# Graph layer on one Trainium2 core: first relu in halves, rank base ahead of the transposes, counts from a column of ones, means on ScalarE in the last phase, last store cut

## The chip, the cores and the metric

One Trainium2 chip, one core of it. The metric is the device time of the whole kernel in microseconds (us).

## The reference

A layer of a graph network on 3,125 nodes of 64 features with 53,125 edges (sorted by destination), float32:

```python
h = relu(layernorm(x))
msg = concatenate([h[dst], edge_attr], axis=1)      # per edge
m = relu(msg @ W1a.T + b1a) @ W1b.T + b1b           # hidden 128
agg = segment_sum(m, src) / maximum(counts(src), 1) # mean per node
z = relu(concatenate([h, agg]) @ W2a.T + b2a) @ W2b.T + b2b
out = x + concatenate([z, h]) @ Wr.T + br
```

## The kernel before

The second matmul of an edge is linear, so the kernel averages the relu'd hidden rows per source node and applies the combined weights `wc` to the mean.

**Edges.** They come in 52 groups of 1,024 (8 tiles of 128), and two groups are a pair. For a pair PE projects windows of `h` (L861), ScalarE copies them into `pw` (L758), DVE makes a one-hot of the destination within a window (`onehot`, L512), and `hidden(g)` (L912) multiplies edges and one-hot with `pw` in 8 calls (16 matmul instructions) into two PSUM banks. `relu(g)` (L766) writes the result into a payload buffer `pay`, one of `PB` = 4.

**Ranks.** The hidden rows must be brought together by source node. Nodes lie in 25 buckets of 125. PE counts for every edge how many edges of its bucket came before it: `ranks_from` (L873) sets the PSUM bank `RANK` to the base of each bucket's region, `ranks_before` and `ranks_on` (both through `count_on`, L876) add counts. DVE's `ranks_b` makes slot numbers of it (L492 to L504, the last being `pos_i`), and writes the node's place in its bucket, 1 to 125, as `MARK` behind the 128 hidden values. POOL then writes each tile with one indirect DMA, a scatter, into `slots_dram` (L411): 8 per group, 416 in all, after `pos` and `rl` of the group. A row there has 144 floats. Regions are cleared beforehand by SP's DMAs (L296), since padding rows must have mark 0. Reuse of a payload buffer waits for its scatters (L500 on DVE, L765 on ScalarE).

**Phases.** The pairs are cut into phases of 8, 8, 6, 3 and 1. When a phase's scatters have landed, its regions are read back bucket by bucket in rounds: SP loads rows (L331, four buffers in turn), DVE compares marks with 1 to 125 (`hots`, L523), PE multiplies (L928, `sum_round`), DVE adds to `sums` (L538). A planner at the top of the function spreads rounds over the group loop by counts of matmuls. What is left comes after the loop (`left_over`).

**The last phase** is nine tails, eight of 3 buckets and one of 1. Each engine writes its order out by hand, in software pipeline. For iteration q, PE does `sum_round(q)`, `transposes(q-1)` (L983), `z1(q-2)` (L993), `outs(q-3)` (L1001). DVE does `hots(q+1)`, `take_tail(q)` (L643 total, L648 to L650 count and reciprocal, L651 mean), `add_z(q-2)` (L660), `add_out(q-3)` (L665). ScalarE copies the transposed mean (L808, for q) and does the relu of z (L814, for q-2). Before, the sum of the column `MARK` is the place times the count, so the count is found with `rec_mark` (reciprocals of 1 to 125) and rounding by `MAGIC`.

**The head.** PE's order is: `transpose_h(0)` (L846), `project_windows(0)` (L861), `ranks_from(0)`, `ranks_before(0)`, `hidden(0)`. SP issues loads and clears in one written order; its load of `dst` for group 3 stands behind many of them.

**Stores.** SP stores the output after tails 3, 6 and 9, each as two DMAs (`HALVES`: partitions 0 to 111 and 112 to 124), L353. A fallback for unusual inputs follows a flag and isn't entered here.

Of the kernel before, what the change touches and what calls it, by code (L numbers as in the profile page):

```python
# [7 lines left out]
def gnn_layer(nc, x_chunks, x, src_cols, dst, dst_blocks, dst_cols, edges_T, w_early, w_late, out):  # L8
# [4 lines left out]
    HID = 128  # L13
# [39 lines left out]
    RW, SW = HID + 16, HID + 1  # L53
    MARK = HID
# [12 lines left out]
    for ph in range(NPH):  # L67
        m = min(3, TPR // C[ph])
        for b0 in range(0, NB, m):
            sum_rounds.append(("sum", ph, b0, min(m, NB - b0)))  # L70
# [37 lines left out]
    with ExitStack() as ctx:  # L108
# [3 lines left out]
        def sem(name):  # L112
# [7 lines left out]
        rec_mark = sb("rec_mark", [128, 1])  # L120
# [88 lines left out]
            oh="onehot_made", H="hidden_made", rl="hidden_relu", pos="slots_ready",  # L209
# [4 lines left out]
            sb="mean_made", sT="mean_transposed", sTe="mean_T_evacuated", z="z_made", za="z_added", zr="z_relu",  # L214
# [48 lines left out]
        OUT_AT = [3, 6, NJ]  # L263
# [4 lines left out]
        def _(sp):  # L268
# [80 lines left out]
            for upto in OUT_AT:  # L349
                hi = tails[upto - 1][1] + tails[upto - 1][2]  # L350
                sp.wait_ge(S["oe"], upto)
                for p0, p1 in HALVES:
                    sp.dma_start(o_v[p0:p1, lo:hi, :], ot[p0:p1, lo:hi, :]).then_inc(S["out"], 16)  # L353
                lo = hi
            sp.wait_ge(S["out"], 16 * len(OUT_AT) * len(HALVES))
# [12 lines left out]
        def _(pool):  # L368
# [29 lines left out]
            count(rec_mark[:], [[0, 1]], 1, 1)  # L398
# [3 lines left out]
            for g in range(NG):  # L402
# [6 lines left out]
                pool.wait_ge(S["rl"], g + 1)  # L409
                for k in range(K):  # L410
                    pool.indirect_dma_start(out=slots_dram[:, :], out_offset=bass.IndirectOffsetOnAxis(ap=pos_i[:, u, k:k + 1], axis=0),  # L411
# [16 lines left out]
        def _(dve):  # L428
# [33 lines left out]
            V.memset(pay[:].rearrange("p u k w -> p (u k) w")[:, :, SW:RW], 0.0).then_inc(S["pad"], 1)  # L462
# [52 lines left out]
            def hots(r):  # L515
# [6 lines left out]
                for t in range(m * C[ph]):  # L522
                    last = V.tensor_scalar(oh2[:, r % 2, t, :], marks[:], rows[:, sum_no[r] % RR, t, MARK:SW], None, ALU.is_equal)  # L523
# [67 lines left out]
            for i in range(NP):  # L591
# [8 lines left out]
                if i == 0:  # L600
# [5 lines left out]
                    dve.wait_ge(S["const"], 4)  # L606
                    link(V.reciprocal(rec_mark[:], rec_mark[:]))
# [32 lines left out]
            def take_tail(q):  # L640
                r, b0, m = tails[q]
                dve.wait_ge(S["ag"], r + 1)
                V.tensor_tensor(tot[:, q % 2, 0:m, :], sums[:, b0:b0 + m, :], summed(r), ALU.add).then_inc(S["tk"], 1)  # L643
                dve.wait_ge(S["tk"], r + 1)
                if q >= 2:
                    dve.wait_ge(S["sT"], q - 1)
                c = cnt[:, q % 2]
                link(V.tensor_scalar(c[:, 0:m, 0], tot[:, q % 2, 0:m, MARK], rec_mark[0:BN, :], MAGIC, ALU.mult, ALU.add))  # L648
                link(V.tensor_scalar(c[:, 0:m, 1], c[:, 0:m, 0], -MAGIC, 1.0, ALU.add, ALU.max))
                link(V.reciprocal(c[:, 0:m, 2], c[:, 0:m, 1]))  # L650
# [447 lines left out]
```

## Time and profile before

| | us |
|---|---|
| median of 3 runs | 594.39 (594.15 to 594.48) |
| profiled execution, its own time | 594.85 |
| span of the profiled execution | 593.1 |
| POOL busy, 442 instructions | 408.2 (69%) |
| PE matmul busy | 383.1 (65%) |
| PE weight load busy | 344.5 (58%) |
| DVE busy | 318.1 (54%) |
| ACT busy | 100.2 (17%) |
| mean granted clock of TensorE | 0.805 |

PE is TensorE (PEld its weight loads, which overlap), DVE is VectorE, ACT ScalarE, POOL GpSimd, SP the engine that issues most DMAs (SPq its queue). The 1.7 us between span and time lie around the span. Shares are of the whole span; what one stage is worth must be read in that stage.

### The profile page before, as it was taken

The page shows a single profiled execution, that of the slowest core. Times are in us where ns is not written, and L with a number is a line of the kernel's source. Part 1 is how long each engine was busy: PE and PEld are TensorE (multiplying, and loading weights), DVE is VectorE, ACT ScalarE, POOL GpSimd, SP SyncE. Part 2 cuts the span into 40 slices and gives each one's busy share as a digit, 9 for nine tenths or more (in the row PEclk, how much of TensorE's full clock was granted, in tenths as well). Part 3 has the DMA queues.
Part 4 walks back from the last instruction along what each step waited for, and adds up shares of the span by engine and source line. Part 5 has one row for each costly group of instructions (what it writes and reads, how often), then busy time and mean ns, then how long its engine had stood idle before and what let it go on. Part 6 is the DMA issues. An engine that isn't in the chain of part 4 may idle for free.

```text
span 593.1 us, 7898 instructions
## 1 busy us (share of the span) xinstructions
PE 383.1 (65%) x2608; PEld 344.5 (58%) x2608; DVE 318.1 (54%) x1237; ACT 100.2 (17%) x145; POOL 408.2 (69%) x442
## 2 busy tenths in 40 slices
PE   5546947976255267378468551763985928897875
PEld 3445847745145267378457551663875928797754
DVE  6658422334233346357446432562765818888895
ACT  2241511112122021022112220211221211100022
POOL 2677777777777777777777777777777777777000
PEclk9775957678676596788789765968896978999999
DMA  8982845363443695677675647858697594969511
GB/s 195 362 233 88 243 136 170 92 187 101 124 132 125 186 290 182 215 242 228 221 230 161 180 137 234 247 184 255 200 305 235 165 309 126 323 216 315 177 38 57
DMA packets 54637, 116.35 MB, mean 196 GB/s; under 512 B 9869, under 2 KB 30949, under 8 KB 54593
## 3 DMA queue, kind: packets, MB, share of 16 engines
q1 hardware_dynamic: 41281, 85.11, 47.8%
q0 software_dynamic: 13312, 30.70, 16.2%
q8 instruction: 22, 0.36, 0.3%
q14 instruction: 22, 0.18, 0.1%
HBM read 68.62 MB, written 47.14 MB: 195 GB/s over the span
## 4 chain that ended last, share of the span: by engine, by line
POOL 42%; issue 18%; PE 15%; DMA 11%; DVE 7%; SPq 3%; ACT 2%; POOLq 0%; DVEq 0%; ACTq 0%
POOL slots_dram L411 42%; DMA slots_dram<-pay,pos_i 7%; PE bank L912 6%; PE bank L928 5%; DVE oh L523 3%; DMA dstb<-in_dst 2%; DMA rows<-slots_dram 2%; ACT pay L766 1%; PE bank L1001 1%; DVE eo L512 1%; PE bank L876 1%; PE bank L861 1%; SPq L272 1%; PE bank L932 1%; ACT z1T L814 1%
## 5 line engine op out<-in xcount | busy, mean ns | idle before, releaser
L411 POOL DMA_INDIRECT slots_dram<-pay,pos_i x416 | 404.2, 972 | 139.5 <-issue 123.5
L912 PE MATMUL bank<-pw,eo 128*128 128x128 f32 x832 | 142.7, 343 | 166.9 <-DVE eo L512 166.1
L912 PEld LDWEIGHTS bank<-pw,eo 128*128 128x128 f32 x832 | 134.4, 253 | 176.5 <-issue 176.1
L928 PE MATMUL bank<-rows,oh 128*125 128x129 f32 x1050 | 126.0, 275 | 9.8 <-DVE oh L523 9.6
L928 PEld LDWEIGHTS bank<-rows,oh 128*125 128x125 f32 x1050 | 119.7, 188 | 13.7 <-issue 12.9
L766 ACT ACTIVATE pay<-bank 128x1024 f32<-128x1024 f32 x52 | 53.3, 1024 | 409.1 <-PE bank L912 407.9
L523 DVE TENSOR_SCALAR oh<-marks,rows 128x125 f32<-128x125 f32 x525 | 108.1, 293 | 3.1 <-DMA rows<-slots_dram 2.5
L501 DVE COPY pay<-mark 128x8 f32<-128x8 f32 x52 | 10.6, 214 | 142.8 <-DMA slots_dram<-pay,pos_i 142.1
L512 DVE TENSOR_SCALAR eo<-dstb,lane 64x256 f32<-64x256 int32 x208 | 64.0, 367 | 6.0 <-DMA dstb<-in_dst 5.2
L492 DVE TENSOR_TENSOR slot_t<-bank,eq 128x416 f32<-128x416 f32 x26 | 15.3, 590 | 48.7 <-PE bank L876 47.4
L861 PE MATMUL bank<-we_in,hT 65*128 65x128 f32 x208 | 38.5, 347 | 0.7 <-ACT hT L751 0.7
L861 PEld LDWEIGHTS bank<-we_in,hT 65*128 65x128 f32 x208 | 36.8, 265 | 1.6 <-issue 1.1
L758 ACT COPY pw<-bank 64x512 f32<-64x512 f32 x52 | 30.0, 578 | 11.2 <-PE bank L861 10.4
L538 DVE TENSOR_TENSOR sums<-sums,bank 125x258 f32<-125x258 f32 (+2 forms) x48 | 20.5, 428 | 13.3 <-PE bank L928 13.3
L876 PE MATMUL bank<-fours,all_rows 128*128 128x312 bf16 (+1 forms) x156 | 24.1, 265 | 0.0
L876 PE MATMUL bank<-eq,below 128*128 128x416 bf16 x26 | 9.6, 371 | 16.2 <-DVE fours L488 16.2
L876 PEld LDWEIGHTS bank<-fours,all_rows 128*128 128x128 bf16 x156 | 14.8, 104 | 1.7
L494 DVE TENSOR_REDUCE pos<-slot_t 128x16 f32<-128x416 f32 x26 | 15.2, 586 | 0.9
L484 DVE TENSOR_TENSOR eq<-srcq,bucket_row 128x416 bf16<-128x416 f32 x26 | 15.2, 586 | 0.4
L876 PE MATMUL bank<-eq,all_rows 128*128 128x208 bf16 x52 | 14.6, 280 | 0.0
L876 PEld LDWEIGHTS bank<-eq,below 128*128 128x128 bf16 x26 | 2.6, 102 | 20.1 <-DVE fours L488 17.1
L876 PE MATMUL bank<-twos,all_rows 128*128 128x208 bf16 x52 | 14.3, 274 | 0.0
(138 smaller groups left out, 225.4 us busy)
## 6 DMA issues: line engine op xcount, KB each, us to landing
rows<-slots_dram SPq DMA_DIRECT2D x24, 864.0 KB, 7.5
dstb<-in_dst SPq DMA_DIRECT2D x52, 256.0 KB, 8.5
eo<-in_edges_T SPq DMA_DIRECT2D x52, 256.0 KB, 3.8
rows<-slots_dram SPq DMA_DIRECT2D x12, 720.0 KB, 7.8
slots_dram<-zeros SPq DMA_DIRECT2D x9, 864.0 KB, 7.7
slots_dram<-pay,pos_i POOLq DMA_INDIRECT x416
rows<-slots_dram SPq DMA_DIRECT2D x8, 648.0 KB, 5.5
slots_dram<-zeros SPq DMA_DIRECT2D x3, 1008.0 KB, 7.4
```

What stands on the lines that cost most here:

```text
L411: pool.indirect_dma_start(out=slots_dram[:, :], out_offset=bass.IndirectOffsetOnAxis(ap=pos_i[:, u, k:k + 1], axis=0), in_=pay[:, u, k, :] ...
L484: link(V.tensor_tensor(eq, q.unsqueeze(2).to_broadcast((128, PK, NQ)), bucket_row[:].unsqueeze(1).to_broadcast((128, PK, NQ)), ALU.is_equal))
L492: V.tensor_tensor(slot_t[:], RANK, eq_all[:, i % 2], ALU.mult).then_inc(S["rs"], 1)
L512: V.tensor_scalar(eo[p, g % EB, a * HB:(a + 1) * HB], dstb[p, g % DB // 2, a * HB:(a + 1) * HB], lane[p, g // 2, a:a + 1], None, ALU.is_eq ...
L523: last = V.tensor_scalar(oh2[:, r % 2, t, :], marks[:], rows[:, sum_no[r] % RR, t, MARK:SW], None, ALU.is_equal)
L538: V.tensor_tensor(sums[:, b0:b0 + m, :], sums[:, b0:b0 + m, :], summed(r), ALU.add).then_inc(S["tk"], 1)
L758: A.copy(pw[p, g % WB, :, :], bank[p, 7, :].rearrange("p (k h) -> p k h", h=HID)).then_inc(S["pc"], 1)
L766: A.activation(pay[:, u, :, 0:HID], bank[:, b:b + 2, :].rearrange("p b (k h) -> p (b k) h", h=HID), ACT.Relu).then_inc(S["rl"], 1)
L861: last = T.matmul(bank[:, 7, c * HID:(c + 1) * HID], hT_all[:, n0:n0 + 2 * WS], we_in[0:D + 1, :], start=True, stop=True, skip_group_check ...
L876: return T.matmul(out, lhsT, rhs, start=False, stop=True, skip_group_check=True)
L912: last = T.matmul(bank[:, 2 * (g % 2) + k // 4, (k % 4) * HID:(k % 4 + 1) * HID], eo[:, u, k * 128:(k + 1) * 128], pw[:, g % WB, a, :], st ...
L928: last = T.matmul(o[0:BN, v * SW:(v + 1) * SW], oh2[:, r % 2, n, :], rows[:, sum_no[r] % RR, n, 0:SW], start=(t == 0), stop=(t == C[ph] - ...
```

## The change

- The relu of group 0 is done in halves: PE signals after the first 4 of 8 calls, ScalarE does that half, and POOL's first four scatters wait for it alone.
- `ranks_from(0)` goes to the front of PE's order.
- A payload row gets a second extra column, `ONE`, set once to 1.0. The sum of it is the count. `rec_mark` and its steps go. A summed row is 130 wide instead of 129, still three to a PSUM bank.
- In the last phase DVE makes only total, maximum and reciprocal; the mean is made on ScalarE, one activation per bucket with the reciprocal as scale. ScalarE's order for iteration q is now relu of z (q-3), copy (q-1), mean (q).
- The output is stored after tails 3, 6, 7 and 9; the last two as one DMA of 125 partitions each, of 3 and 4 buckets.

The diff, without the semaphore names and the fallback:

```diff
     SLOTS = sum(C) * NB * 128
-    RW, SW = HID + 16, HID + 1
-    MARK = HID
+    RW, SW = HID + 16, HID + 2
+    MARK, ONE = HID, HID + 1
...
     for ph in range(NPH):
-        m = min(3, TPR // C[ph])
+        m = min(512 // SW, TPR // C[ph])
         for b0 in range(0, NB, m):
...
         place = sb("place", [128, 1])
-        rec_mark = sb("rec_mark", [128, 1])
         marks = sb("marks", [128, BN])
...
         NJ = len(tails)
-        OUT_AT = [3, 6, NJ]
+        OUT_AT = [3, 6, NJ - 2, NJ]
+        OUT_PARTS = [HALVES, HALVES, [(0, BN)], [(0, BN)]]
...
             lo = 0
-            for upto in OUT_AT:
+            for upto, parts in zip(OUT_AT, OUT_PARTS):
                 hi = tails[upto - 1][1] + tails[upto - 1][2]
                 sp.wait_ge(S["oe"], upto)
-                for p0, p1 in HALVES:
+                for p0, p1 in parts:
                     sp.dma_start(o_v[p0:p1, lo:hi, :], ot[p0:p1, lo:hi, :]).then_inc(S["out"], 16)
                 lo = hi
-            sp.wait_ge(S["out"], 16 * len(OUT_AT) * len(HALVES))
+            sp.wait_ge(S["out"], 16 * sum(len(parts) for parts in OUT_PARTS))
             sp.wait_ge(S["flag"], 1)
...
             count(block_no[:], [[1, 2]], 0, 2)
-            count(rec_mark[:], [[0, 1]], 1, 1)
             count(marks[:], [[1, BN]], 1, 0).then_inc(S["const"], 1)
...
                 pool.wait_ge(S["pos"], g + 1)
-                pool.wait_ge(S["rl"], g + 1)
+                if g == 0:
+                    pool.wait_ge(S["rl_half"], 1)
+                else:
+                    pool.wait_ge(S["rl"], g + 1)
                 for k in range(K):
+                    if g == 0 and k == K // 2:
+                        pool.wait_ge(S["rl"], 1)
                     pool.indirect_dma_start(out=slots_dram[:, :], out_offset=bass.IndirectOffsetOnAxis(ap=pos_i[:, u, k:k + 1], axis=0),
...
             V.memset(hT_all[:, PAD_L + N:PAD_L + N + PAD_R], 0.0).then_inc(S["hp"], 1)
-            V.memset(pay[:].rearrange("p u k w -> p (u k) w")[:, :, SW:RW], 0.0).then_inc(S["pad"], 1)
+            V.memset(pay[:].rearrange("p u k w -> p (u k) w")[:, :, SW:RW], 0.0)
+            V.memset(pay[:].rearrange("p u k w -> p (u k) w")[:, :, ONE:SW], 1.0).then_inc(S["pad"], 1)
             center(0)
...
                 for t in range(m * C[ph]):
-                    last = V.tensor_scalar(oh2[:, r % 2, t, :], marks[:], rows[:, sum_no[r] % RR, t, MARK:SW], None, ALU.is_equal)
+                    last = V.tensor_scalar(oh2[:, r % 2, t, :], marks[:], rows[:, sum_no[r] % RR, t, MARK:ONE], None, ALU.is_equal)
                 last.then_inc(S["oh2"], 1)
...
                         limits(ph)
-                    dve.wait_ge(S["const"], 4)
-                    link(V.reciprocal(rec_mark[:], rec_mark[:]))
                 if i == 1:
...
                 dve.wait_ge(S["ag"], r + 1)
+                if q >= 2:
+                    dve.wait_ge(S["sb"], q - 1)
                 V.tensor_tensor(tot[:, q % 2, 0:m, :], sums[:, b0:b0 + m, :], summed(r), ALU.add).then_inc(S["tk"], 1)
                 dve.wait_ge(S["tk"], r + 1)
-                if q >= 2:
-                    dve.wait_ge(S["sT"], q - 1)
                 c = cnt[:, q % 2]
-                link(V.tensor_scalar(c[:, 0:m, 0], tot[:, q % 2, 0:m, MARK], rec_mark[0:BN, :], MAGIC, ALU.mult, ALU.add))
-                link(V.tensor_scalar(c[:, 0:m, 1], c[:, 0:m, 0], -MAGIC, 1.0, ALU.add, ALU.max))
-                link(V.reciprocal(c[:, 0:m, 2], c[:, 0:m, 1]))
-                V.tensor_tensor(sbar[:, q % 2, 0:m, :], tot[:, q % 2, 0:m, 0:HID], c[:, 0:m, 2].unsqueeze(2).to_broadcast((BN, m, HID)),
-                                ALU.mult).then_inc(S["sb"], 1)
+                link(V.tensor_scalar(c[:, 0:m, 0], tot[:, q % 2, 0:m, ONE], 1.0, None, ALU.max))
+                V.reciprocal(c[:, 0:m, 1], c[:, 0:m, 0]).then_inc(S["rec"], 1)
...
+            def relu_first_group():
+                act.wait_ge(S["H_half"], 1)
+                A.activation(pay[:, 0, 0:K // 2, 0:HID], bank[:, 0, :].rearrange("p (k h) -> p k h", h=HID), ACT.Relu).then_inc(S["rl_half"], 1)
+                act.wait_ge(S["H"], 1)
+                A.activation(pay[:, 0, K // 2:K, 0:HID], bank[:, 1, :].rearrange("p (k h) -> p k h", h=HID), ACT.Relu).then_inc(S["rl"], 1)
+
             def late_weights():
...
             copy_window(1)
-            relu(0)
+            relu_first_group()
             relu(1)
...
-            for q in range(NJ + 2):
+            def mean(q):
+                r, b0, m = tails[q]
+                act.wait_ge(S["rec"], q + 1)
+                if q >= 2:
+                    act.wait_ge(S["sT"], q - 1)
+                for v in range(m):
+                    last = A.activation(sbar[:, q % 2, v, :], tot[:, q % 2, v, 0:HID], ACT.Copy, scale=cnt[:, q % 2, v, 1:2])
+                last.then_inc(S["sb"], 1)
+
+            def mean_T(q):
+                r, b0, m = tails[q]
+                act.wait_ge(S["sT"], q + 1)
+                if q >= 2:
+                    act.wait_ge(S["z"], q - 1)
+                A.copy(sbarT[:, q % 2, 0:m * BN], bank[:, 7, 0:m * BN]).then_inc(S["sTe"], 1)
+
+            def relu_z(q):
+                r, b0, m = tails[q]
+                act.wait_ge(S["za"], q + 1)
+                if q >= 2:
+                    act.wait_ge(S["o"], q - 1)
+                A.activation(z1T[:, q % 2, 0:m * BN], zt[:, q % 2, 0:m * BN], ACT.Relu).then_inc(S["zr"], 1)
+
+            for q in range(NJ + 3):
+                if 3 <= q:
+                    relu_z(q - 3)
+                if 1 <= q <= NJ:
+                    mean_T(q - 1)
                 if q < NJ:
-                    r, b0, m = tails[q]
-                    act.wait_ge(S["sT"], q + 1)
-                    if q >= 2:
-                        act.wait_ge(S["z"], q - 1)
-                    A.copy(sbarT[:, q % 2, 0:m * BN], bank[:, 7, 0:m * BN]).then_inc(S["sTe"], 1)
-                if q >= 2:
-                    r, b0, m = tails[q - 2]
-                    act.wait_ge(S["za"], q - 1)
-                    if q >= 4:
-                        act.wait_ge(S["o"], q - 3)
-                    A.activation(z1T[:, q % 2, 0:m * BN], zt[:, q % 2, 0:m * BN], ACT.Relu).then_inc(S["zr"], 1)
+                    mean(q)
...
-            transpose_h(0)
-            pe.wait_ge(s_w[0], 16)
-            pe.wait_ge(S["ones"], 3)
-            project_windows(0)
-
             def ranks_from(ph):
                 T.matmul(RANK, ones_row[:], base[:, ph, :].unsqueeze(1).to_broadcast((1, PK, NQ)), start=True, stop=True, skip_group_check=True)
+
+            pe.wait_ge(S["ones"], 3)
+            pe.wait_ge(S["const"], 3)
+            ranks_from(0)
+            transpose_h(0)
+            pe.wait_ge(s_w[0], 16)
+            project_windows(0)
...
                                     pw[:, g % WB, a, :], start=True, stop=True, skip_group_check=True)
+                    if g == 0 and k == K // 2 - 1:
+                        last.then_inc(S["H_half"], 1)
                 last.then_inc(S["H"], 1)
...
-            pe.wait_ge(S["const"], 3)
-            ranks_from(0)
             ranks_before(0)
```

## Rows read from the trace of the kernel before

**Rows 1.** Page, costliest groups: line, engine, op, tiles; busy us, mean ns; idle before.

```profile
L411 POOL DMA_INDIRECT slots_dram<-pay,pos_i x416 | 404.2, 972 | 139.5 <-issue 123.5
```

**Rows 2.** Waits: engine, line, waited for; us in total, times, longest.

```profile
POOL slots_dram L411 <- ACT pay L766: 15.4, 9, 13.0
```

**Rows 3.** Timeline, 4 to 19 us: start us, duration us, instruction, idle before.

```profile
4.10 0.29 POOL L394 TENSOR_SCALAR_AFFINE_SELECT not_below<-not_below 128x128 bf16<-128x128 bf16 x1
...
6.10 0.60 PE L846 MATMUL bank<-ident,xch 125*64 125x125 f32 x2 [6.10 <-DVE xch L456]
...
9.33 1.75 PE L873 MATMUL bank<-base,ones_row 1*128 1x416 f32 x2
...
9.43 1.18 ACT L758 COPY pw<-bank 64x512 f32<-64x512 f32 x2 [2.34 <-PE bank L861]
...
11.01 0.53 PE L876 MATMUL bank<-eq,below 128*128 128x416 bf16 x1
...
12.20 3.74 PE L912 MATMUL bank<-pw,eo 128*128 128x128 f32 x16
...
14.25 0.16 DVE L504 TENSOR_TENSOR pos_i<-pos,beyond 128x8 int32<-128x8 f32 x1
...
15.98 1.02 ACT L766 ACTIVATE pay<-bank 128x1024 f32<-128x1024 f32 x1 [5.36 <-PE bank L912]
...
17.90 1.13 POOL L411 DMA_INDIRECT slots_dram<-pay,pos_i  x1 [12.97 <-ACT pay L766]
```

**Rows 4.** Chain that ended last, 0 to 100 us: start us, duration us, what.

```profile
21.77 12.67 DMA dstb<-in_dst
...
55.52 1.03 ACT pay L766
...
56.65 0.96 POOL slots_dram L411
...
60.43 0.62 POOL slots_dram L411
```

**Rows 5.** The chain, 470 to 594 us.

```profile
485.74 4.09 DMA slots_dram<-pay,pos_i
...
543.09 2.23 PE bank L928 x18
```

**Rows 6.** Timeline, 568 to 579 us.

```profile
569.37 0.87 PE L1001 MATMUL bank<-w2r,z1T 128*125 128x64 f32 x6 [0.34 <-ACT z1T L814]
...
575.20 0.87 PE L1001 MATMUL bank<-w2r,z1T 128*125 128x64 f32 x6 [0.34 <-ACT z1T L814]
575.43 0.23 DVE L648 TENSOR_SCALAR cnt<-tot,rec_mark 125x3 f32<-125x3 f32 x1
575.69 0.17 DVE L649 TENSOR_SCALAR cnt<-cnt 125x3 f32<-125x3 f32 x1
...
576.11 0.56 DVE L651 TENSOR_TENSOR sbar<-tot,cnt 125x384 f32<-125x384 f32 x1
576.59 0.54 DVE L660 TENSOR_TENSOR zt<-bank,zh 128x375 f32<-128x375 f32 x1
...
577.67 0.52 ACT L814 ACTIVATE z1T<-zt 128x375 f32<-128x375 f32 x1
...
578.24 0.87 PE L1001 MATMUL bank<-w2r,z1T 128*125 128x64 f32 x6 [0.34 <-ACT z1T L814]
```

**Rows 7.** Windows: us, busy us of each engine (instructions), granted clock, DMA share, GB/s.

```profile
560.00:588.30 28.30, 22.60 (x140) 16.00 (x137) 25.38 (x89) 7.77 (x18) 0.00 (x0) 1.00 0.23 64
589.00:590.50 1.50, 0.00 (x0) 0.00 (x0) 0.00 (x0) 0.00 (x0) 0.00 (x0) 0.91 0.58 171
```

**Rows 8.** Groups of instructions, all lines.

```profile
L772 ACT ACTIVATE z_bias<-bank,wl 128x1 f32<-128x1 f32 x1 | 0.3, 277 | 0.0
```

**Rows 9.** Timeline of SP, 588 to 594 us.

```profile
588.27 0.76 SPq L353 DMA_DIRECT2D out<-xs  x2
```

**Rows 10.** Waits of SP's queue, 440 to 600 us.

```profile
SPq L357 <- DMA out<-xs: 1.4, 1, 1.4
```

More of the change, by code:

```diff
@@ L208, in gnn_layer @@
             wm="weights_combined", we="combined_evacuated",
-            oh="onehot_made", H="hidden_made", rl="hidden_relu", pos="slots_ready",
+            oh="onehot_made", H="hidden_made", rl="hidden_relu", H_half="first_half_hidden_made", rl_half="first_half_hidden_relu", pos="slots_ready",
             rc="row_counts", rk="ranks_made", rs="ranks_read", rkd="ranks_moved_on", rkf="ranks_checked",
@@ L213, in gnn_layer @@
             xh="h_part_made", xhe="h_part_added", zh="z_h_made", zhe="z_h_evacuated",
-            sb="mean_made", sT="mean_transposed", sTe="mean_T_evacuated", z="z_made", za="z_added", zr="z_relu",
+            rec="reciprocal_counts", sb="mean_made", sT="mean_transposed", sTe="mean_T_evacuated", z="z_made", za="z_added", zr="z_relu",
             o="out_made", oe="out_added", out="out_stored", flag="flag_set")
@@ L717, in _ @@
                         dve.wait_ge(L["oe"], b)
-                    step(V.tensor_scalar(cnt[:, 0, 0, 1:2], sums[:, b, MARK:SW], 1.0, None, ALU.max))
+                    step(V.tensor_scalar(cnt[:, 0, 0, 1:2], sums[:, b, MARK:ONE], 1.0, None, ALU.max))
                     step(V.reciprocal(cnt[:, 0, 0, 2:3], cnt[:, 0, 0, 1:2]))
-                    step(V.tensor_scalar(cnt[:, 0, 0, 3:4], sums[:, b, MARK:SW], 0.5, None, ALU.is_lt))
+                    step(V.tensor_scalar(cnt[:, 0, 0, 3:4], sums[:, b, MARK:ONE], 0.5, None, ALU.is_lt))
                     V.tensor_scalar(sbar[:, 0, 0, :], sums[:, b, 0:HID], cnt[:, 0, 0, 2:3], None, ALU.mult).then_inc(L["mean"], 1)
```

## The prediction

> **What bounds the kernel now.** I began with the page's costliest groups. The POOL group is the one to see [rows 1]: 416 scatters of 972 ns and 123.5 us of issue between them (0.30 each), a period of some 1.26 us that runs on from the first scatter at 17.9 [rows 3] and fills most of the span. The waits of POOL [rows 2] say that it is hardly ever short of work: of 15.4 us spent on relus 13.0 is the wait for the first group, the other eight share 2.4. So the kernel has three pieces: a **head** until POOL's first scatter, POOL's train, and an **end** after the scatters.
>
> In the timeline of the head [rows 3] the reader is to see one serial chain for group 0. In the timeline and the chain around group 4 [rows 4] the thing to see is a deadline. Scatters can be counted: group 4's first is POOL's 33rd, at 60.43, and its relu ended at 55.52 + 1.03 = 56.55, 3.88 us ahead. I laid all 52 groups side by side so: after the first, this margin is the smallest. From the sixties on the ring of four payload buffers ties every group to the landing of older scatters [rows 5], so whatever shifts POOL shifts all of it, up to the landing at 489.8 from which the chain runs through DVE and PE to the end.
>
> The last phase is nine tails (eight of three buckets, one of one). Its rows [rows 6] show a period of 3.04 us between outs (575.20 and 578.24). PE stands idle 0.34 us in each before outs, for ScalarE's relu; DVE's rows name no idle time. So DVE is the bound and PE is close behind it: over 28.30 us it has 22.60 busy against DVE's 25.38, at a granted clock of 1.00 [rows 7].
>
> **Part 1, the head.** The change moves the base of the ranks (two matmuls, 9.33 to 11.01, so 1.68 us [rows 3]) from between the window projection and the rank counts to the very front of PE. It waits there for POOL's last constants, ready at 4.10 + 0.29 = 4.39, and ends at 4.39 + 1.68 = 6.07; the transposes queued behind it started at 6.10, when DVE's h was ready. I cost the move at 0 (from 0 to 0.3 if the first matmul starts slowly). Without it there everything behind moves up by 1.68: hidden starts at 12.20 - 1.68 = 10.52, positions are ready at 14.25 + 0.16 - 1.68 = 12.73. DVE's one-hots and ScalarE's window copy (9.43, half of 1.18 for group 0, so 10.02) are ready before 10.52 and are the next cover: at most 0.5 us more can be had.
>
> The half relu: hidden's 16 matmuls take 3.74, the first eight half of it, 1.87, so 12.39. The relu of 512 instead of 1,024 elements is not in the trace; between 0.51 (half of 1.02) and 1.02. Nearest is the window copy of 512 elements, 0.59: done at 13.0. POOL began 0.90 after its relu's end (15.98 + 1.02 = 17.00 to 17.90), so now at 13.9: **4.0 earlier**. The second half's relu ends near 14.26 + 0.6, and POOL wants it four scatters later, at 19.0: its extra wait costs 0. Behind that wait on POOL stand only later scatters.
>
> What is late next: group 4. Its chain doesn't pass through group 0. It starts with a dst load that SP issued at 21.77 and that took 12.67 us to land, then DVE, then hidden and relu until 56.55 [rows 4]. POOL would now want it at 60.43 - 4.0 = 56.4. The chain takes the scatter at 56.65 for released by this relu, though it is the 30th and belongs to group 3: POOL's queue runs three scatters ahead of its engine. So from relu to scatter it takes between 0.1 (56.55 to 56.65) and 0.9 [rows 3, 4]. Group 4 would start between 56.65 and 57.45 if its relu stays. The dst load shares its engines with three more scatters than before, which can add 0 to 1.3 (a tenth of 12.67). So POOL's train is ahead by 60.43 minus 56.65 to 58.75, **1.7 to 3.8, and I take 3.0**. From there the shift is passed on whole.
>
> **Part 2, the mean on ScalarE.** DVE loses two of three small steps' worth and the product: from the start of the first to the start of the z addition 575.43 to 576.59 is 1.16 us [rows 6]. Left are a maximum and a reciprocal, as the last two small steps now from 575.69 to 576.11, 0.42: 0.74 less. DVE's own sequence falls to 2.30, and the 0.34 of PE's idle time is what the period can give: 3.04 - 0.34 = **2.70**, with PE the bound. ScalarE gets three activations of 128 elements with a scale from a tile. The trace has none. The one row with an operand from a tile takes 0.28 for a single element [rows 8]; a relu of 375 elements takes 0.52 [rows 6]. Between these I take 0.32, near the first, so 0.97 for three. With a relu of 0.52 and a copy of the same 375 elements at no more than that, ScalarE is busy 2.0 of 2.70: a cover 0.7 us wide.
>
> By the Trainium skill (ScalarE: Activation LUTs, What ACT_TABLE_LOAD costs) a [128,1] pointer adds about 93 ns to 186 ns + 0.833 ns per element, and neighbours overlap by 93 ns: 0.39 + 2 x 0.29 = 0.97 us, an estimate. The trace agrees where it can: 0.28 for one element [rows 8].
>
> Order matters too: is the mean late? Counted from a tail's sum on PE at t, which takes 0.7, I estimate DVE's total to end near t + 1.5 (0.5 and a little queueing), the reciprocal t + 1.95, the mean t + 2.9; its transposes come at t + 2.7 + 0.8 = t + 3.5. Relu and copy stand in front of the mean, for older tails; their inputs are there by t + 1.1. So 0.6 us to spare, and no wait replaces the old one in the steady part.
>
> The first tails gain more, since PE has no outs yet and DVE alone sets the pace: three times 0.74, less what the mean's chain is longer (0.97 against DVE's 0.56 and a hand-over), 2.2 - 0.6 = 1.6 by the first outs, 569.37 before. From there to the sixth outs five periods at 0.34 are 1.7, less 0.1 for the short last one. The last two tails are a latency chain of like length. **Tail: 3.1**, from 2.0 (the early gain lost) to 3.7.
>
> **Part 3, width.** Each row summed is 130 wide, not 129, on PE and DVE. Eighteen matmuls of 129 columns take 2.23 us [rows 5], 124 ns each, so one column is about 1 ns; some 200 on the path after 490 us, with DVE's additions: **+0.3**, from 0 to 0.5. The buckets per round stay three (512 // 130). The memset of ones falls before x arrives, DVE's reciprocal of marks and POOL's iota go from places with slack: 0.
>
> **Part 4, the stores.** Now two DMAs go out in 0.76 us of SP after DVE's end, and SP waits 1.4 more [rows 9, 10]. Then one goes, 0.38 less, and with 128 KB instead of 219. One of 125 partitions isn't in the trace. Spread as before it wins 0.38 + 0.3 = 0.7. If only few engines take it, it costs: the 219 KB occupied 16 engines for 1.50 x 0.58 us [rows 7], 13.9 engine-us or at most 0.11 per row of 1,792 B; 25 rows on one engine, of 1,024 B, are 25 x 0.06 to 0.11 = 1.6 to 2.8 against 8 x 0.11 = 0.9 now, so from +0.3 to +1.5 after the 0.38. I take **0**, between the ends. The added third store goes out before the last tails' outs are added and takes 0.4 of SP: 0.
>
> The Trainium skill (DMA: Bandwidth & Descriptors, Why a DMA increments its semaphore by 16 and not by 1) says that a DMA from SP uses the largest number of engines up to 16 that divides the slowest dimension: for 125 that is 5, against 16 and 13 for the halves of before. It speaks against this edit; by it this term is about +0.5 and the time 589.1. No row here shows it.
>
> **Sum** against the profiled execution: 594.85 - 3.0 - 3.1 + 0.3 + 0 = 589.05. The median of the runs is 0.46 below the profiled one, so **588.6**.
>
> **Rivals.**
> - *Group 4 eats the head's gain.* For it: the margin is under 4 us and the dst load took 12.67. Against: that load isn't touched. Head 0.8 instead of 3.0: 590.8. Chance 0.14.
> - *The tail only changes its bound*: the mean is late in most tails and PE waits for it before its transposes as it did for the relu. Against: 0.6 us to spare. Tail 0.8: 590.9. Chance 0.12.
> - *The store on five engines*, a mechanism beside the others: 25 rows in line on each. About half likely by the bounds above; with the forecast's other terms 588.9 to 590.1. I count it inside the forecast, at 0.3 of its 0.64.
> - *The change does nothing visible*, both hold: 594.0. Chance 0.05.
> - *Slower: ScalarE becomes the tail's bound.* If an activation with a scale costs 1.02, like the relu of 1,024, ScalarE needs 3.06 + 1.04 = 4.1 per tail against 3.04: nine times 1.06 is +9.5, less the head's 3.0, plus 0.3: 601.2. It decides against the tail's gain from (3.04 - 1.04) / 3 = 0.67 us per activation, and against the whole change from 0.8; no row suggests that much. Chance 0.03.
> - *Everything at its better end*: head 3.8, tail 3.7, stores 0.7 gained: 586.5. Chance 0.02.
>
> **The numbers.** Forecast 0.64. Bounds of the terms: head 1.7 to 3.8, tail 2.0 to 3.7, stores -0.7 to +1.5 give 594.39 - 3.8 - 3.7 + 0.3 - 0.7 = 586.5 at the one side, and I go to 586.4; on the other I go to 591.4, which takes in the first two rivals. A measurement of this kernel tells 0.2% (1.2 us) from no change. Faster takes the forecast, the first two rivals and the better end, 0.92, less 0.01 that goes to slower; same is the case of nothing visible, 0.05; slower 0.04.
>
> **What would show it.** First scatter near 13.9 and base of ranks ending before the transposes, which stay near 6.1; group 4's first scatter near 57.4 with POOL idle before it; last scatter about 3 earlier; tail period 2.70 with PE's idle time gone, three activations of some 0.3; out 3 us sooner against the last scatter. Wrong would be: transposes delayed over 0.3, a POOL wait of over 2 us at group 4, transposes waiting for ScalarE in every tail, or over 2.5 us from the last store's issue to its landing.

## The result and the profile after

| us | before | after |
|---|---|---|
| median of 4 runs, same chip | 594.43 (594.15 to 595.43) | 588.22 (586.08 to 589.49) |
| profiled execution, its own time | 594.85 | 586.08 |
| span | 593.1 | 584.4 |
| first scatter | 17.90 | 13.95 |
| end of the last scatter | 548.60 | 545.74 |
| first transposes of a tail | 562.27 | 558.89 |
| end of the last out addition | 588.24 | 579.59 |
| from there to the end of the span | 4.86 | 4.81 |

The ratio is 0.9871, with an interval of 0.9846 to 0.9897: faster by 1.3%, or 6.2 us. One thing stands out before any reading: the profiled execution is the fastest of the four, 2.1 us below the median. So the trace explains 8.8 us, and the median shows 6.2. Medians and ratios here and below are of fast runs: one run of before, of 617.44 us at a granted clock of 0.616, is left out.

The **head** after, as the timeline has it (start us, duration us, instruction, idle before):

```profile
4.11 0.29 POOL L394 TENSOR_SCALAR_AFFINE_SELECT not_below<-not_below 128x128 bf16<-128x128 bf16 x1
...
4.55 1.72 PE L891 MATMUL bank<-base,ones_row 1*128 1x416 f32 x2 [4.55 <-POOL not_below L394]
...
6.20 0.63 PE L869 MATMUL bank<-ident,xch 125*64 125x125 f32 x2
...
10.38 3.63 PE L937 MATMUL bank<-pw,eo 128*128 128x128 f32 x16
...
12.45 0.60 ACT L770 ACTIVATE pay<-bank 128x512 f32<-128x512 f32 x1 [1.86 <-PE bank L937]
...
13.95 1.13 POOL L415 DMA_INDIRECT slots_dram<-pay,pos_i  x1 [9.10 <-ACT pay L770]
```

The base of the ranks now lies in front of the transposes, which start 0.10 later than before; hidden starts at 10.38 (12.20 before), the half relu takes 0.60, and POOL starts 3.95 earlier than in [rows 3].

Then the **deadline of group 4**, in the same timeline between 54 and 59 us:

```profile
54.02 0.95 POOL L415 DMA_INDIRECT slots_dram<-pay,pos_i  x1 [0.30 <-issue]
...
55.18 1.02 ACT L766 ACTIVATE pay<-bank 128x1024 f32<-128x1024 f32 x1 [11.99 <-PE bank L937]
...
56.98 0.96 POOL L415 DMA_INDIRECT slots_dram<-pay,pos_i  x1 [2.00 <-ACT pay L766]
```

POOL stands idle 2.00 us instead of the 0.30 of issue: the relu ends at 56.20, 0.35 earlier than before, and the scatter follows 0.78 later. Group 4 starts at 56.98 against 60.43 [rows 4]: of 3.95 us the train keeps 3.45.

The **last phase** after: two steady tails, from the timeline.

```profile
568.59 0.76 PE L1026 MATMUL bank<-w2r,z1T 128*125 128x64 f32 x6
568.64 0.18 DVE L652 RECIPROCAL cnt<-cnt 125x3 f32<-125x3 f32 x1
568.79 0.55 DVE L660 TENSOR_TENSOR zt<-bank,zh 128x375 f32<-128x375 f32 x1
568.86 0.99 ACT L814 ACTIVATE sbar<-tot,cnt 125x128 f32<-125x128 f32 x3 [0.23 <-DVE cnt L652]
...
569.19 0.88 PE L955 MATMUL bank<-rows,oh 128*125 128x130 f32 x6
...
569.75 0.50 ACT L829 ACTIVATE z1T<-zt 128x375 f32<-128x375 f32 x1
...
569.91 0.53 PE L1008 MATMUL bank<-ident,sbar 125*128 125x125 f32 x3
...
570.27 0.80 PE L1018 MATMUL bank<-sbarT,wc 128*128 128x375 f32 x2
570.48 0.47 ACT L822 COPY sbarT<-bank 128x375 f32<-128x375 f32 x1 [0.22 <-PE bank L1008]
...
570.91 0.77 PE L1026 MATMUL bank<-w2r,z1T 128*125 128x64 f32 x6
```

PE has no idle time left in these tails, and the three activations take 0.99. DVE has none either: its z additions start at 568.79 and 571.13 (2.34 apart), and every one of its instructions between them follows the one before without a wait. So the trace doesn't say which of the two sets the new pace. The outs come at 563.88, 566.20, 568.59, 570.91 and 573.31: a period of (573.31 - 563.88) / 4 = 2.36, against 3.04 before and a forecast of 2.70. The **store's** rows of after, first the wait, then windows that follow its issue at 579.62 (columns as in [rows 2] and [rows 7]):

```profile
SPq L357 <- DMA out<-xs: 2.3, 1, 2.3
```

```profile
580.50:580.80 0.30, 0.00 (x0) 0.00 (x0) 0.00 (x0) 0.00 (x0) 0.00 (x0) 0.50 0.30 92
580.80:581.10 0.30, 0.00 (x0) 0.00 (x0) 0.00 (x0) 0.00 (x0) 0.00 (x0) 0.50 0.30 61
581.10:581.40 0.30, 0.00 (x0) 0.00 (x0) 0.00 (x0) 0.00 (x0) 0.00 (x0) 0.50 0.32 106
```

The DMA share is 0.30 to 0.32, and 5 of 16 engines is 0.31: the 125 rows go out through five engines. SP waits 2.3 us for them instead of 1.4 [rows 10]. Yet SP isn't the last engine to finish. POOL's last instruction is a DRAIN of 2.68 us, here beside SP's (ns of one, then its start):

```profile
L108 POOLq DRAIN  x1: 2682/2682/2682, 580.7 to 580.7; - x1
L108 SPq DRAIN  x1: 13/13/13, 583.3 to 583.3; - x1
```

POOL's ends 3.77 us after the last out addition, in before as in after; SP gets to its own after 3.33 us in before and 3.73 in after. The longer wait of the store is hidden behind POOL.

### The profile page after: what moved, and what is told of

Same layout as the page of the kernel before. It is cut to its first block, busy times and chain, and to the rows that moved or that the text cites. A ratio compares the mean times of both kernels' runs of the same rounds, so it can differ in the third digit from the quotient of the medians.

```text
span 584.4 us, 7910 instructions
## 1 busy us (share of the span) xinstructions
PE 377.0 (65%) x2608; PEld 341.6 (58%) x2608; DVE 312.9 (54%) x1219; ACT 108.0 (18%) x171; POOL 407.5 (70%) x441
## 4 chain that ended last, share of the span: by engine, by line
POOL 45%; issue 19%; PE 16%; DVE 7%; DMA 7%; SPq 3%; ACT 2%; POOLq 0%; DVEq 0%
POOL slots_dram L415 45%; PE bank L955 7%; PE bank L937 5%; DMA slots_dram<-pay,pos_i 4%; DVE oh L528 3%; DMA dstb<-in_dst 2%; DMA rows<-slots_dram 1%; DVE eo L517 1%; ACT pay L766 1%; PE bank L901 1%; PE bank L884 1%; SPq L320 1%; PE bank L1026 1%; PE bank L1018 1%; SPq L272 1%
## 5 line engine op out<-in xcount | busy, mean ns | idle before, releaser
L955 PE MATMUL bank<-rows,oh 128*125 128x130 f32 x1050 | 126.8, 276 | 8.4 <-DVE oh L528 8.2
L517 DVE TENSOR_SCALAR eo<-dstb,lane 64x256 f32<-64x256 int32 x208 | 65.3, 374 | 8.2 <-DMA dstb<-in_dst 7.4
L884 PE MATMUL bank<-we_in,hT 65*128 65x128 f32 x208 | 36.1, 331 | 0.5 <-issue 0.5
L884 PEld LDWEIGHTS bank<-we_in,hT 65*128 65x128 f32 x208 | 34.6, 251 | 1.4 <-issue 0.9
L543 DVE TENSOR_TENSOR sums<-sums,bank 125x260 f32<-125x260 f32 (+2 forms) x48 | 20.6, 429 | 11.3 <-PE bank L955 10.9
L814 ACT ACTIVATE sbar<-tot,cnt 125x128 f32<-125x128 f32 x25 | 8.3, 392 | 33.2 <-DVE cnt L652 33.1
```

The costliest lines, as they stand in the source:

```text
L517: V.tensor_scalar(eo[p, g % EB, a * HB:(a + 1) * HB], dstb[p, g % DB // 2, a * HB:(a + 1) * HB], lane[p, g // 2, a:a + 1], None, ALU.is_eq ...
L543: V.tensor_tensor(sums[:, b0:b0 + m, :], sums[:, b0:b0 + m, :], summed(r), ALU.add).then_inc(S["tk"], 1)
L884: last = T.matmul(bank[:, 7, c * HID:(c + 1) * HID], hT_all[:, n0:n0 + 2 * WS], we_in[0:D + 1, :], start=True, stop=True, skip_group_check ...
L955: last = T.matmul(o[0:BN, v * SW:(v + 1) * SW], oh2[:, r % 2, n, :], rows[:, sum_no[r] % RR, n, 0:SW], start=(t == 0), stop=(t == C[ph] - ...
```

## The experiments

My theory on the result: the head's shift arrives less 0.5 at group 4, the last phase gives 5.3 because PE had more room than its idle time shows, and the store is a wash. The rivals are: the edits help each other; the store costs; executions differ because of something that the one trace lacks.

### The edits apart

**Head alone**: before, with the half relu and the base in front.

```diff
-            relu(0)
+            relu_first_group()
...
+            ranks_from(0)
+            transpose_h(0)
```

> The head's edits alone on the kernel before (half relu, base of ranks first). Theory, a deadline at group 4: first scatter at 13.95, POOL's train 4 to 5 us ahead until group 3, group 4's first scatter held at 57 by its relu, and 2.9 to 3.4 us of the lead left at the last scatter: 591.2 (590.5 to 592.0). Rival A, nothing is held and the whole lead is passed on: 589.4 to 590.4. Rival B, the head's lead is lost by the end and the tail's edit made the whole gain: 593.5 or more.

Measured: 593.50 (12 runs; before on that chip 594.89), ratio 0.9975 (0.9955 to 0.9994), so 0.4 to 2.7 us faster. The time missed the expected 590.5 to 592.0 and is the one that rival B named. But the trace speaks against B's mechanism, since the lead is there at the last scatter. It has the first scatter at 13.94, group 4's at 57.13 after an idle time of 2.25, the last scatter's end 3.29 earlier than before's, and a span of 589.9 against 593.1. From the first transposes of a tail to the last addition it takes 25.97, as before. This profiled execution took 591.63, 1.9 less than its median, so again the trace shows more than the runs.

**Last phase alone**: the column of ones, the mean on ScalarE; half relu, base of the ranks and stores as before.

```diff
-                V.tensor_tensor(sbar[:, q % 2, 0:m, :], tot[:, q % 2, 0:m, 0:HID], c[:, 0:m, 2].unsqueeze(2).to_broadcast((BN, m, HID)),
-                                ALU.mult).then_inc(S["sb"], 1)
+                V.reciprocal(c[:, 0:m, 1], c[:, 0:m, 0]).then_inc(S["rec"], 1)
```

> The last phase's edits alone on the kernel before (column of ones, mean on ScalarE in the new order), stores as before. Theory, the tail gives more than I forecast because PE's matmuls go by faster once nothing waits: period of a tail 2.36 to 2.40 instead of 3.04, last scatter where it was (547.6), 5.4 less: 589.0 (588.3 to 589.8). Rival, the tail gives the forecast 3.1 less 0.3 and the rest of the gain seen comes from the head: period 2.70, 591.6.

Measured: 590.52 (6 runs), ratio 0.9920 (0.9895 to 0.9944), 3.3 to 6.2 us faster; the median lies above the expected 588.3 to 589.8. First transposes at 562.97, last addition's end at 583.67: 20.70, against 25.97. That is 5.27 less, and the same 20.70 stands in the trace of after (579.59 - 558.89). The head of this trace wasn't quite as before: `hidden(0)` took 3.10 instead of 3.74 with the same instructions, and the first scatter came at 17.19, 0.7 earlier; its last scatter still ended at 550.05, 1.45 later. The two medians lie 1.4 and 4.4 below before's, together 5.8, beside 6.2 for the whole change. Within intervals of over 2 us each that is a sum; the traces say it more sharply (3.29 and 5.27, with 8.8 for both). No sign is left of edits that need each other.

**The two head edits singly**, one run each.

> The half relu alone on the kernel before. Hidden starts at 12.20 as before, its first half ends at 14.07, half relu 0.60, positions ready 14.41: first scatter 15.5 to 15.7. Rival, POOL waits for positions or needs longer to start when its wait is met early: 16.5 or later.

> The base of the ranks alone moved to PE's front, on the kernel before. Everything behind it 1.7 to 1.8 earlier, the transposes not more than 0.15 later than 6.10: first scatter 16.1 to 16.3. Rival, the transposes or the window projection are late by what it takes (1.7): first scatter 17.9.

Measured: the half relu alone puts the first scatter at 15.77 (2.1 earlier), the base alone at 15.88 (2.0 earlier). Their times are 594.96 and 594.70 beside a before of 596.24 on that chip. Both lie just outside the expected ranges, by 0.1 and by 0.2. With the base alone `hidden(0)` starts at 10.38, 1.82 earlier, and takes 3.54 instead of 3.74, which gives the other 0.2. The half relu doesn't wait for that end. So 2.13 and 1.82 are what adds up, and their 3.95 is what both together gave.

### The order on ScalarE

The mean ahead of the relu and the copy, as a first thought would write it:

```diff
             for q in range(NJ + 3):
+                if q < NJ:
+                    mean(q)
                 if 3 <= q:
                     relu_z(q - 3)
                 if 1 <= q <= NJ:
                     mean_T(q - 1)
-                if q < NJ:
-                    mean(q)
```

> The changed kernel with ScalarE's order in the last phase turned round: the mean first, then the relu of z and the copy. Theory: the relu waits for a reciprocal it doesn't need, so it ends near t + 3.4 after a tail's sum on PE and outs come behind it; period 4.0 instead of 2.36, span 10 to 14 us longer. Rival, the order is indifferent since ScalarE is busy only 2 us per tail: period 2.36 to 2.5.

Measured: 600.26, beside 596.05 for before: slower than before. Its ScalarE, from the timeline:

```profile
574.48 0.98 ACT L814 ACTIVATE sbar<-tot,cnt 125x128 f32<-125x128 f32 x3 [2.54 <-DVE cnt L652]
575.37 0.50 ACT L829 ACTIVATE z1T<-zt 128x375 f32<-128x375 f32 x1
575.78 0.45 ACT L822 COPY sbarT<-bank 128x375 f32<-128x375 f32 x1
```

ScalarE is idle for 2.54 us before 574.48, with a relu queued behind the mean whose input DVE had added by 570.62. PE's outs wait for that relu, the next sum stands behind outs, and the next mean waits for that sum: a loop. First transposes to last addition take 32.36 (560.84 to 593.20) instead of 20.70: +11.7, with the same 0.98 for three activations. Not all of it is the order. The windows show the clock (third from the end):

```profile
566.00:571.00 5.00, 2.81 (x18) 1.94 (x17) 2.76 (x9) 2.54 (x8) 0.00 (x0) 1.00 0.15 44
571.00:575.00 4.00, 3.36 (x17) 2.56 (x17) 1.83 (x7) 1.46 (x5) 0.00 (x0) 0.73 0.00 0
575.00:580.00 5.00, 4.39 (x18) 3.69 (x17) 2.40 (x8) 1.33 (x5) 0.00 (x0) 0.53 0.19 58
```

At a clock of 1.00 the period is 4.21 (outs at 567.43 and 571.64), 1.85 more than 2.36; the one of 5.42 (575.92 to 581.34) lies mostly in the slow stretch. So some 1.2 of the 11.7 in that period alone is the clock's, and a second slow stretch from 586.5 to 589.9 adds a little. Between 9 and 10 are the order's (an estimate: 1.6 by the first outs and 1.85 for each of the four periods behind them, and most of the rest): enough to turn a gain of 5.3 into a loss. The expected period (4.0) and lengthening (10 to 14) came.

### The last store

The changed kernel with its last store cut in two again (112 and 13 partitions):

```diff
-        OUT_PARTS = [HALVES, HALVES, [(0, BN)], [(0, BN)]]
+        OUT_PARTS = [HALVES, HALVES, [(0, BN)], HALVES]
```

> The changed kernel with the last store cut into halves again (112 and 13 partitions), the third left as one DMA of 125. Theory, one DMA of 125 partitions uses 5 of the 16 engines: two issues of 0.38 each but SP's wait for the output falls from 2.3 to about 1.1 to 1.3, DMA share in the last stretch up from 0.3 to over 0.5: 0.7 faster than the changed kernel (0.4 to 1.0). Rival, the 125 rows are spread over 16 engines and the 2.3 is something else: 0.3 to 0.4 slower.

Measured: 589.03 (6 runs, 588.04 to 589.81), ratio 0.9895 (0.9872 to 0.9918). The wait, in the waits of SP's queue:

```profile
SPq L357 <- DMA out<-xs: 1.1, 1, 1.1
```

So cutting takes 1.2 us off the wait, for one issue more: SP gets to its last instruction 3.01 us after the last addition instead of 3.73, the 0.7 that I expected. But the kernel doesn't end sooner: from the last addition to the end are 5.06 us (4.81 in after). The reason stands in the same view as before:

```profile
L108 POOLq DRAIN  x1: 2682/2682/2682, 584.0 to 584.0; - x1
L108 SPq DRAIN  x1: 13/13/13, 585.9 to 585.9; - x1
```

POOL's DRAIN ends 3.77 us after the last addition, as in every trace here (within 0.01), and SP's wait lies within it. The last DRAINs of all are PE's or DVE's, between 4.5 and 5.3 us after the addition in the thirteen traces; what they wait for isn't shown. So the cut shortens the wait as expected, and the wait isn't what ends the kernel: SP is 0.7 earlier, and the end is 0.25 later. The changed kernel wasn't timed on this chip, and the ratio lies between the two that it had on others (0.9871, and 0.9916 below), so no gain is resolved.

### What makes group 4 late

In after's trace DVE clears `sums` from 43.37 for 2.77 us (L615, in pair 1), ahead of the ranks and one-hots of group 4. Moved to pair 4:

```diff
-                    V.memset(sums[:], 0.0).then_inc(S["sz"], 1)
...
+                if i == 4:
+                    V.memset(sums[:], 0.0).then_inc(S["sz"], 1)
```

> The changed kernel with DVE's memset of sums (2.75 us, in group 4's chain) moved three pairs later. Theory, group 4 is POOL's deadline: its relu ends some 2.7 earlier (53.5), POOL does not stall there, group 4's first scatter comes at 54.7 to 55.3, and the time falls by 1.5 to 2.3. Rival A, the stall at group 4 comes from somewhere else (clearing of regions, which group 4 also waits for): no change. Rival B, the memset costs in its new place what it saves: 0 to 0.5 less.

Measured: 588.87 (6 runs), ratio 0.9889 (0.9866 to 0.9913). POOL's first scatter of group 4:

```profile
56.38 1.05 POOL L415 DMA_INDIRECT slots_dram<-pay,pos_i  x1 [0.31 <-issue]
```

The relu of group 4 ends at 54.38 instead of 56.20, not at the expected 53.5, and the idle time is gone. Why 1.8 and not 2.8 stands in DVE's rows where it waits for the `dst` load that the prediction named, in after and then in this run:

```profile
34.39 1.27 DVE L517 TENSOR_SCALAR eo<-dstb,lane 64x256 f32<-64x256 int32 x4 [7.39 <-DMA dstb<-in_dst]
```

```profile
35.46 1.32 DVE L517 TENSOR_SCALAR eo<-dstb,lane 64x256 f32<-64x256 int32 x4 [8.80 <-DMA dstb<-in_dst]
```

The load came 1.07 later this time. From this one-hot to the start of group 4's hidden it takes 17.27 us in after (51.66) and 14.11 here (49.57), so the clearing is worth 3.2 of the chain, and the load's landing moves all of it. In the eleven traces with the clearing in its old place that distance is 17.25 to 17.38, while the one-hot starts anywhere from 33.95 to 35.72. So group 4 is late by both: its chain begins with the load, and the clearing lies in it. Group 4 starts only 0.6 earlier (54.7 to 55.3 was expected), as in this execution four scatters took 1.23 to 1.57 instead of 0.96, and the last scatter ends at 546.44, later than in after's trace. The expected 1.5 to 2.3 less in time isn't shown: this ratio, too, lies between the changed kernel's two. Then came something that the traces of before and after don't show, in the windows (granted clock is the third number from the end):

```profile
553.00:556.40 3.40, 3.40 (x19) 3.40 (x19) 2.44 (x12) 0.00 (x0) 0.00 (x0) 0.54 0.22 63
```

For 3.4 us TensorE runs at the lower of its two levels (0.54 is the mean of a window that it nearly fills). Before it, PE stood idle for 2.30 us, waiting for a one-hot behind a late read-back. The trace with the last store cut has such a stretch from 563.4 to 566.8, after two idle times of 0.91 and 0.78, and there first transposes to last addition take 21.97, 1.3 more than in after.

### The changed kernel again, and the best version

On another chip, unaltered, beside a version with both edits (clearing moved, last store cut).

> The changed kernel once more, unaltered, to place the others beside it on one chip. The theory that head and tail add (3.3 and 5.3 in the traces) says 8 to 8.6 less than the kernel before in an execution whose clock stays at 1.00 from 495 us on, first scatter 13.95, POOL idle before group 4 for about 2 us, tail period 2.36, wait for the output 2.3. If the first profile was a lucky one, this trace lacks one of these. Timed: 0.987 of before, 0.984 to 0.990.

> The changed kernel with both repairs: memset of sums three pairs later, last store in halves. Theory (deadline at group 4, and 5 of 16 engines for 125 partitions): no idle time of POOL before group 4, wait for the output 1.1, together 1 to 2.5 less than the changed kernel. Rival, from the two single runs: a lower granted clock between 550 and 567 us takes it away again, so 0 to 1 less in the median, and the trace shows a stretch at 0.50 there.

| median us (runs) | us | ratio to before |
|---|---|---|
| before (11) | 596.24 (594.37 to 597.51) | |
| changed (6) | 591.01 (589.24 to 591.74) | 0.9916 (0.9898 to 0.9935) |
| both edits more (6) | 588.94 (587.65 to 591.18) | 0.9881 (0.9859 to 0.9903) |

The change is worth 5.2 us here, 6.2 in the first measurement; the ratio lies outside the 0.984 to 0.990 that I expected. The version with both edits has the lower median by 2.1, but the intervals overlap; it's likely better, not shown to be. The profiled execution of the changed kernel starts its scatters at 13.95, as in the first trace, yet ends them at 548.15, 2.4 later: the same instructions, a longer train. Of that 1.3 is group 4, which starts at 58.29 instead of 56.98 after 2.25 us of idle time, mostly since the `dst` load came 1.02 later. The other 1.1 are scatters behind it that took longer. Two long scatters are easy to see ahead of group 4, where they cost nothing, as POOL would only have waited longer:

```profile
38.44 1.77 POOL L415 DMA_INDIRECT slots_dram<-pay,pos_i  x1 [0.30 <-issue]
...
43.04 1.57 POOL L415 DMA_INDIRECT slots_dram<-pay,pos_i  x1 [0.30 <-issue]
```

and DVE in the same stretch:

```profile
38.15 1.23 DVE L446 TENSOR_TENSOR xch<-xs,stat 125x1024 f32<-125x1024 f32 x1
...
42.55 1.23 DVE L460 TENSOR_TENSOR xch<-xch,stat 125x1024 f32<-125x1024 f32 x1
```

Each long scatter starts while a DVE operation with two inputs in SBUF is running. They take 0.8 and 0.6 us longer than 0.96, and each ends 0.83 us after that operation: 38.44 + 1.77 = 40.21 against 38.15 + 1.23 = 39.38, and 44.61 against 43.78. In all thirteen traces every scatter over 1.2 us meets such an operation.

### Do two-input DVE operations hold scatters?

Four extra DVE operations in each of pairs 4 to 19, of like length: once with two SBUF inputs (the edit below), once with one, as the control (a tensor_reduce of `srcq`). Their result is overwritten unread.

```diff
+                if 4 <= i < 20:
+                    for extra in range(4):
+                        link(V.tensor_tensor(slot_t[:].rearrange("p k b -> p (k b)"), srcq[:].rearrange("p g k -> p (g k)"), limit[:].rearrange("p g k -> p (g k)"), ALU.max))
```

> The changed kernel with 4 more VectorE operations per pair in 16 pairs (64 in all), each a tensor_tensor of 416 elements with two SBUF inputs into scratch, put where VectorE is idle waiting for scatters. Theory: POOL's scatters are held while VectorE runs an operation with two SBUF inputs, so scatters of over 1.2 us become frequent (one or two per pair) and POOL's train gets 10 to 24 us longer. Rival, the slow scatters are chance or DMA traffic: train as in the changed kernel (530 to 532), time within 2 us.

> Control: the same 64 extra VectorE operations in the same places, of the same length (about 0.59), but tensor_reduce with a single SBUF input. Theory of held scatters: no more slow scatters than in the changed kernel, train 530 to 532. Rival, it is VectorE's time as such that delays POOL: the same lengthening as with two inputs.

Measured: first to last scatter 534.21 with two inputs, 531.32 in the control; times 590.33 and 587.77, one run each. Of the difference of 2.9, 0.4 is there when group 4 starts, before the added operations begin (58.58 against 58.15). The other 2.5 are longer scatters: the pauses between them sum to 116.8 in both. Nine scatters that met an added operation with two inputs took 1.01 to 1.30 instead of 0.96, none in the control. One of them, POOL and then DVE:

```profile
165.61 1.30 POOL L415 DMA_INDIRECT slots_dram<-pay,pos_i  x1 [0.30 <-issue]
```

```profile
165.49 2.46 DVE L599 TENSOR_TENSOR slot_t<-srcq,limit 128x416 f32<-128x416 f32 x4
```

The kind is confirmed, the size missed: I had expected 10 us or more, and the nine holds sum to 2.2. By the Trainium skill (SBUF — State Buffer, SBUF: two separate sides) a DVE operation with two SBUF inputs holds a port pair against a GpSimd operation that reads SBUF, and the loser waits for the whole instruction. The rows agree on which operations collide, and they show what the loser waits for: the scatter at 165.61 ends at 166.91, 0.83 after the first of the four operations, which ends at 166.07.

How often it costs is no chance. In the thirteen timelines 154 scatters start within one of three such operations: `eq` from `srcq` and the probe's `slot_t` (0.59 each), and the two that make `xch` of 1,024 elements (1.23). Of the 95 that start with more than 0.16 us of it left, 91 end 0.83 us after it; the other four start in its first 0.04 and take 0.96. Those with less left take 0.95 to 0.99. So a scatter that starts behind the operation, and early enough in it, is held up to its end, and 0.83 us of its own follow. Nine scatters started in that part of an added operation with two inputs, and all nine were held; in the control fifteen started 0.10 to 0.40 into an added one, and none was. That a hold is rare is the timing of this loop: most scatters started near the end of the operation (19 of the 29 that started within an added one, 0.47 or more into it). The train's length alone would not have shown it, since from group 4's start to the end of the last scatter the thirteen traces lie between 488.1 and 491.4, and the probe's 490.6 is among them.

## Why the prediction was right, and where it wasn't

588.6 was forecast, 588.22 measured; the first rival's and the second's terms didn't come, and ScalarE as the slower bound didn't either. The closeness is better than the working deserves, and is luck: two misses cancel. By the medians of the edits apart the head gave 1.4 (0.4 to 2.7) where 3.0 were forecast, and the last phase 4.4 (3.3 to 6.2) where 3.1 less 0.3 were. In the traces the head's term is about right and the tail's is too small, and it is the difference of one execution from another that takes the surplus back.

- **Head to the first scatter**: 13.9 forecast, 13.95 measured. The half relu took 0.60 (bounds 0.51 to 1.02, taken as 0.59), and the transposes were 0.10 late. Right.
- **Group 4**: start forecast between 56.65 and 57.45, measured 56.98, as the relu moved by 0.35 and the scatter followed 0.78 later. The lead is 3.45, inside 1.7 to 3.8 and 0.45 over what I took. The reason that I gave for its lateness, the `dst` load, was right and incomplete: the chain begins there, and DVE's clearing lies in it with 3.2. POOL's wait was 2.00 here and 2.25 in the second trace, where I had named over 2 as a sign of being wrong; the lead that I forecast already held such a wait, so the sign was badly set.
- **"From there the shift is passed on whole"**: in the profiled execution yes (last scatter 2.86 earlier, first transposes 3.38). In time only partly: the head alone is worth 0.4 to 2.7 us over 12 runs. Why isn't settled. The train of the same kernel differed by 2.4 us between two traces (1.3 at group 4, mostly by the later `dst` load, and 1.1 by longer scatters), so the shift is there, under noise of its own size.
- **Tail, the step that failed**: "the 0.34 of PE's idle time is what the period can give". It gave 0.68. PE's starts show where: from z1's to outs' start 1.14 before and 0.64 now, 0.50 less, of which the profile had called 0.34 idle; from outs to sum 0.70 and now 0.60; the rest lies around sum and transposes. Part of the wait for the relu had been hidden within z1's modelled 0.80: now outs start 0.64 after z1, inside that row. By parts: first outs 2.1 sooner (1.6 forecast), the next five periods 2.96 (1.6), the end 0.2 (0). So 5.27, against a 3.1 with an upper bound of 3.7 (the prediction's two parts of 1.6 in fact sum to 3.2). That ScalarE is covered and the old wait isn't replaced was right. That PE is then the bound isn't shown: I had DVE's own sequence at 2.30 and PE's at 2.70, and the measured 2.36 lies next to DVE's, with no idle time on either.
- **Activations**: 0.97 forecast for three, 0.98 measured. The margin of the order was right too: as written PE waits for a mean only in the first two tails (0.91 and 0.78), not in the steady ones; with the mean in front the period is 4.21.
- **Width**: +0.3 can't be seen apart; six matmuls of 130 columns take 0.88, as six of 129 did.
- **Store**: 0 forecast, -0.05 measured. The Trainium skill's rule that the prediction quoted (DMA: Bandwidth & Descriptors) gave five engines, and five it is. For SP the net cost of about +0.5 came, too: it gets to its last instruction 0.4 later. It isn't in the time because POOL's DRAIN of 2.68 covers it, a row that the prediction left out. So the term was right for a wrong reason, and the 0.7 to be won at its better end wasn't to be had. From the store's issue to the end of SP's wait are 2.6 us, over the 2.5 that I had named as a sign of being wrong.
- **Execution to execution**: nothing in the sum stood for it. I put the median 0.46 below the profiled execution, as it was before; after, it lies 2.1 above. The sum for the profiled execution was 589.05 and it took 586.08, 2.97 too high: 2.2 from the tail, 0.4 from the head, and the 0.3 of width that can't be seen. The 2.6 between the two offsets brought the median back to the forecast.
- **A sum of the rivals**: with both held (head 0.8, tail 0.8, width 0.3) the time is 594.39 - 1.6 + 0.3 = 593.1, not 594.0.

What makes the other three executions slower stays open. Three things that vary were seen: the landing of the `dst` load that starts group 4's chain (33.9 to 35.7 over the traces); how many scatters are held behind it; and stretches at the lower clock in the last 40 us, in the traces of four versions of the changed kernel (store cut, clearing moved, the two together, and the turned order). The three slower runs had mean granted clocks of 0.799, 0.799 and 0.804, the profiled one 0.813, which would fit the third. But of the six later runs of the same kernel the slowest (591.74) had 0.814 and the fastest (589.24) 0.806, so the mean clock doesn't decide it.

## What to carry to other kernels

Where the profile models an engine's ends, read its room from start to start between instructions and not from the idle time named: a wait can be hidden in the row before it. When work moves to a third engine in a pipeline written by hand, put it behind what older iterations still need; the same three activations went with a gain of 5 us in the last place and with a loss in the first. And when the expected effect is near 1%, one profiled execution is one draw: compare a trace's gain with the medians before believing a term to a tenth. And before shortening the last wait of one engine, look at when the others finish.

## What the runs showed of the hardware

- A scatter of POOL (0.96) that starts within a DVE operation with two SBUF inputs, with more than 0.16 us of it left, ends 0.83 us after that operation: 91 of 95 in thirteen traces, and the other four started in its first 0.04. They take up to 1.37 with operations of 0.59 and up to 1.77 with those of 1.23. With one SBUF input none of fifteen was held.
- A store of 125 partitions ran at a DMA share of 0.30 to 0.32 and was waited for 2.3 us; cut in 112 and 13 it was 1.1, for one more issue.
- POOL's DRAIN at the end of this program took 2.68 us and ended 3.8 us after the last out addition in all thirteen traces; SP, done with its wait for the output, came to its own DRAIN after 3.0 to 3.75.
- After idle times of 0.8 to 2.3 us on PE in an otherwise busy stretch, four traces show 3.4 us or more at a granted clock of 0.50. The trace of after has idle times of 0.91 and 0.78 at the same place in the work and stays at 1.00, as do four others, so what decides isn't shown.
